# Tile 3's gram split by columns, and tile 2's layers moved ahead of its last rows, in a recommendation tower on one core

## The reference

```python
e = stack([tbl_f[ids[:, f]] for f in range(26)], axis=1)
T = concatenate([r_dense[:, None, :], e], axis=1)
Z = einsum('bnd,bmd->bnm', T, T)
z = Z[:, iu0, iu1]                       # upper triangle, 351 numbers
h = concatenate([z, r_dense], axis=1)    # 479
h = maximum(h @ W_top1 + b_top1, 0.0)    # 512
h = maximum(h @ W_top2 + b_top2, 0.0)    # 256
y = h @ W_top3                           # 1
```

## Time and profile before

| | us |
|---|---|
| median of 3 runs (lowest, highest) | 124.29 (123.7, 124.66) |
| the profiled execution's own time | 124.55 |
| its span in the trace | 122.6 |
| busy: PE, PE's weight load | 93.3, 76.8 |
| busy: DVE, ACT, POOL | 75.5, 73.7, 75.4 |
| mean granted clock of TensorE | 0.956 of full |

### The profile page before, as it was taken

How to read it: one execution, slowest core, us unless ns; L and a number is a source line. 1 busy time by engine, 2 the same in 40 slices (tenths; PEclk the granted TensorE clock), 3 DMA queues, 4 the chain that set the end, 5 groups by cost and what they waited for, 6 DMA issues and landing times. The chain is left out here.

```text
span 122.6 us, 3575 instructions
## 1 busy us (share of the span) xinstructions
PE 93.3 (76%) x1460; PEld 76.8 (63%) x1460; DVE 75.5 (62%) x164; ACT 73.7 (60%) x154; POOL 75.4 (62%) x82
## 2 busy tenths in 40 slices
PE   5659988979789879956519798787947666579791
PEld 5547755646557658756408697676937456569680
DVE  4979999999999995036350993119920104880422
ACT  4097799998799978378380997209942105860000
POOL 4888777887887887787878787777878600040000
PEclk9999999999999999998555999999999999999999
DMA  1896786969899831121222122121222100000000
GB/s 50 244 311 214 259 262 203 289 184 275 184 241 345 267 85 43 43 70 47 66 61 70 50 67 62 51 64 48 64 62 65 48 21 5 8 19 1 0 5 0
DMA packets 7452, 13.64 MB, mean 111 GB/s; under 512 B 2378, under 2 KB 4108, under 8 KB 7308
## 3 DMA queue, kind: packets, MB, share of 16 engines
q1 hardware_dynamic: 5068, 8.67, 22.6%
q0 software_dynamic: 2368, 4.74, 14.3%
HBM read 13.16 MB, written 0.00 MB: 107 GB/s over the span
## 5 line engine op out<-in xcount | busy, mean ns | idle before, releaser
L301 POOL DMA_INDIRECT rows<-tbl,idx x72 | 73.3, 1018 | 22.9 <-issue 21.6
L353 PE MATMUL l<-hot,t_hi 128*128 128x512 f32 x68 | 29.4, 433 | 6.2 <-DVE hot L537 3.8
L537 DVE TENSOR_TENSOR hot<-ids_bc,rownum 128x512 fp32r<-128x512 int32 x51 | 32.3, 693 | 0.4 <-PE l L355 0.4
L355 PE MATMUL l<-hot,t_lo 128*128 128x512 f32 x68 | 28.1, 414 | 0.0
L419 DVE COPY Zlow<-gr 14x224 f32<-14x224 f32 x16 | 8.6, 540 | 22.2 <-PE gr L370 22.0
L353 PEld LDWEIGHTS l<-hot,t_hi 128*128 128x128 f32 x68 | 13.7, 201 | 13.5 <-issue 7.9
L370 PE MATMUL gr<-XT 128*32 128x26 f32 x1024 | 14.8, 202 | 8.4 <-issue 4.9
L370 PEld LDWEIGHTS gr<-XT 128*32 128x32 f32 x1024 | 12.7, 117 | 11.2 <-issue 7.0
L502 ACT COPY XT<-tp 128x512 f32<-128x512 f32 (+1 forms) x20 | 12.2, 654 | 10.6 <-PE tp L341 10.5
L341 PE MATMUL tp<-ident,rows 128*128 128x128 f32 x72 | 11.4, 295 | 7.4 <-DMA rows<-tbl,idx 3.7
L419 ACT COPY Zlow<-gr 14x224 f32<-14x224 f32 x16 | 8.7, 545 | 13.1 <-PE gr L370 12.9
(11 more groups left out here) (32 smaller groups left out, 62.5 us busy)
## 6 DMA issues: line engine op xcount, KB each, us to landing
ids_bc<-ids_oh SPq DMA_DIRECT2D x8, 256.0 KB, 4.1
table<-small SPq DMA_DIRECT2D x4, 512.0 KB, 4.1
table<-small SPq DMA_DIRECT2D x2, 640.0 KB, 5.6
rows<-tbl,idx POOLq DMA_INDIRECT x72, 3.2
w_sb<-w SPq DMA_DIRECT2D x1, 1024.0 KB, 8.6
table<-small SPq DMA_DIRECT2D x2, 320.0 KB, 5.4
w_sb<-w SPq DMA_DIRECT2D x1, 512.0 KB, 8.2
table<-small SPq DMA_DIRECT2D x2, 192.0 KB, 4.9
```

The source lines that it names most:

```text
L301: nc.gpsimd.indirect_dma_start(rows[:, t, place - FIRST, :], None, tbls[f], bass.IndirectOffsetOnAxis(ap=idx[:, t, f:f + 1], axis=0)).then ...
L353: nc.tensor.matmul(lookup_bank(i), t_hi[:, i % PARTS, c * D:(c + 1) * D], hot[:, k % HOTS, :], start=c == 0, stop=False)
L355: last = nc.tensor.matmul(lookup_bank(i), t_lo[:, i % PARTS, c * D:(c + 1) * D], hot[:, k % HOTS, :], start=False, stop=c == n - 1)
L537: nc.vector.tensor_tensor(hot[:, k % HOTS, :], ids_bc[:, i % IDS, :], rownum[:, v, c:c + 1].broadcast_to((OH_ROWS, BATCH)), ALU.is_equal). ...
```

## The change

- The groups of every tile are now 4, 4, 4, 3 and 3 places.
- Tile 3's gram: `gram 3 h` takes places 0 to 20 alone and waits for the first three groups. Two new steps `late 3 h` follow when the last two groups are in: 64 matmuls each, weights of 27 places, six columns moving. Of the eight Zt copies of an engine for each half, four stay with the gram and four go to the late step. The five moves of Zlow wait for the first part alone.
- Tile 2's layers now stand ahead of tile 3's gram; tile 0's and 1's layers stand between grams and rows steps in a new order, each layer1 in two halves apart.
- Tile 3's dense part (`layer1 3 0`) follows the late matmuls and no longer has layer2 of tile 2 behind it. Blocks 0 and 1 go to the banks of `tp`.
- Tile 3's ReLUs are shared: DVE blocks 0 and 2, ACT 1 and 3; of the second layer's two one each.
- The weights of a gram are 27 (tile 3: 21) places, not 32.

```diff
-GROUPS = [(a, min(4, PLACES - a)) for a in range(FIRST, PLACES, 4)]
+LATE_QUADS = 2
+LATE = PLACES - LATE_QUADS * CHUNKS
+GROUPS = [(a, min(4, LATE - a)) for a in range(FIRST, LATE, 4)] + [(a, CHUNKS) for a in range(LATE, PLACES, CHUNKS)]
...
+    steps += [("rows", 1, 0), ("rows", 1, 1)]
+    steps += [("gram", 0, 0), ("rows", 1, 2), ("gram", 0, 1), ("rows", 1, 3), ("rows", 1, 4)]
+    steps += [("gram", 1, 0), ("rows", 2, 0), ("layer1", 0, 0), ("gram", 1, 1), ("layer1", 0, 1), ("rows", 2, 1),
+              ("layer2", 0, 0), ("rows", 2, 2), ("layer1", 1, 0), ("rows", 2, 3), ("layer1", 1, 1), ("rows", 2, 4)]
+    steps += [("gram", 2, 0), ("layer2", 1, 0), ("gram", 2, 1), ("rows", 3, 0), ("rows", 3, 1), ("layer1", 2, 0),
+              ("rows", 3, 2), ("layer1", 2, 1), ("layer2", 2, 0), ("gram", 3, 0), ("gram", 3, 1), ("rows", 3, 3), ("rows", 3, 4)]
+    steps += [("late", 3, 0), ("late", 3, 1), ("layer1", 3, 0), ("layer1", 3, 1), ("layer2", 3, 0)]
...
                 elif kind == "gram":
-                    pe.wait_ge(tp_empty, banks_filled(("rows", t, len(GROUPS) - 1)))
+                    pe.wait_ge(tp_empty, banks_filled(("rows", t, len(GROUPS) - 1 - (LATE_QUADS if t == TILES - 1 else 0))))
+                    n = LATE if t == TILES - 1 else PLACES
...
-                            last = nc.tensor.matmul(gr[PAD * s:PAD * (s + 1), halves % GRAM_BANKS, q, 0:FIELDS],
-                                                    XT[:, b, :], XT[:, b, 1:PLACES], start=True, stop=True)
+                            last = nc.tensor.matmul(gr[PAD * s:PAD * s + n, halves % GRAM_BANKS, q, 0:n - 1],
+                                                    XT[:, b, 0:n], XT[:, b, 1:n], start=True, stop=True)
...
+                elif kind == "late":
+                    pe.wait_ge(tp_empty, banks_filled(("rows", t, len(GROUPS) - 1)))
+                    pe.wait_ge(gram_dve, halves - GRAM_BANKS + 1)
+                    pe.wait_ge(gram_act, halves - GRAM_BANKS + 1)
+                    for q in range(QH):
+                        for s in range(SAMPLES):
+                            b = t * P + (i * SAMPLES + s) * QH + q
+                            last = nc.tensor.matmul(gr[PAD * s:PAD * s + PLACES, halves % GRAM_BANKS, q, 0:PLACES - LATE],
+                                                    XT[:, b, 0:PLACES], XT[:, b, LATE:PLACES], start=True, stop=True)
...
                 elif kind == "layer1" and t == TILES - 1 and i == 0:
                     pe.wait_ge(gram_dve, HALVES * TILES)
                     pe.wait_ge(gram_act, HALVES * TILES)
+                    pe.wait_ge(tp_empty, banks)
...
                 elif kind == "layer1" and t == TILES - 1:
+                    pe.wait_ge(gram_dve, HALVES * (TILES + 1))
+                    pe.wait_ge(gram_act, HALVES * (TILES + 1))
...
+                elif kind == "late":
+                    act.wait_ge(gram_full, halves + 1)
+                    copy_high(nc.scalar.copy, t, i, halves % GRAM_BANKS, range(SAMPLES - ACT_SAMPLES, SAMPLES),
+                              range(QUADS - LATE_QUADS, QUADS), LATE - 1).then_inc(gram_act, 1)
...
+                elif kind == "layer1" and t == TILES - 1 and i == 1:
+                    act.wait_ge(l2_full, t)
+                    for u in range(1, BLOCKS, 2):
+                        act.wait_ge(l1_full, t + 1 + u)
+                        nc.scalar.activation(h1[:, u, :], l1_block(t, u), ACT.Relu).then_inc(h1_act, 1)
```

More of the change, by code:

```diff
@@ L100, in timeline @@
         steps += [("rows", 0, g) for g in ROWS_AFTER.get(i, [])]
[L101 to L111, removed]
+    steps += [("rows", 1, 0), ("rows", 1, 1)]
[5 more added lines that the diff above has]
+    steps += [("late", 3, 0), ("late", 3, 1), ("layer1", 3, 0), ("layer1", 3, 1), ("layer2", 3, 0)]
+    return steps
 STEPS = timeline()
@@ L413, in _, with copy_low @@
                     last.then_inc(l3_full, 1)
-        def copy_gram(copy, t, h, half, samples, low_copied):
+        def copy_low(copy, t, h, bank, samples):
             for s in samples:
@@ L419, in copy_gram, with copy_high, early_quads @@
                 last = copy(Zlow[:, t % 2, :, first:first + QH].rearrange("n m q -> n q m"),
-                            gr[PAD * s:PAD * s + LOW, half, :, 0:LOW])
-            last.then_inc(low_copied, 1)
+                            gr[PAD * s:PAD * s + LOW, bank, :, 0:LOW])
+            return last
+        def copy_high(copy, t, h, bank, samples, quadrants, column):
             for s in samples:
                 first = t * P + (h * SAMPLES + s) * QH
-                for g, n in enumerate(HIGH_ROWS):
+                for g in quadrants:
+                    n = HIGH_ROWS[g]
                     last = copy(Zt[PAD * g:PAD * g + n, :, first:first + QH].rearrange("n c q -> n q c"),
-                                gr[PAD * s:PAD * s + n, half, :, n - CHUNKS:n])
+                                gr[PAD * s:PAD * s + n, bank, :, n - CHUNKS - column:n - column])
             return last
+        def early_quads(t):
+            return range(QUADS - (LATE_QUADS if t == TILES - 1 else 0))
         @block.scalar
@@ L505, in _ @@
                     banks += 1
+                elif kind == "layer1" and t == TILES - 1 and i == 1:
[3 more added lines that the diff above has]
+                        nc.scalar.activation(h1[:, u, :], l1_block(t, u), ACT.Relu).then_inc(h1_act, 1)
+                elif kind == "layer2" and t == TILES - 1:
+                    act.wait_ge(w2_in, 2 * 16)
+                    act.wait_ge(l3_full, t)
+                    act.wait_ge(l2_full, t + 1)
+                    nc.scalar.activation(h2[:, 1, :], l2_block(t, 1), ACT.Relu,
+                                         bias=tail_sb[:, 0, 1:2]).then_inc(h2_act, 1)
         @block.vector
@@ L545, in _ @@
                     dve.wait_ge(gram_full, halves + 1)
-                    copy_gram(nc.vector.tensor_copy, t, i, halves % GRAM_BANKS,
-                              range(SAMPLES - ACT_SAMPLES), low_dve).then_inc(gram_dve, 1)
+                    samples = range(SAMPLES - ACT_SAMPLES)
+                    copy_low(nc.vector.tensor_copy, t, i, halves % GRAM_BANKS, samples).then_inc(low_dve, 1)
+                    copy_high(nc.vector.tensor_copy, t, i, halves % GRAM_BANKS, samples, early_quads(t),
+                              0).then_inc(gram_dve, 1)
+                    halves += 1
+                elif kind == "late":
+                    dve.wait_ge(gram_full, halves + 1)
+                    copy_high(nc.vector.tensor_copy, t, i, halves % GRAM_BANKS, range(SAMPLES - ACT_SAMPLES),
+                              range(QUADS - LATE_QUADS, QUADS), LATE - 1).then_inc(gram_dve, 1)
                     halves += 1
@@ L555, in _ @@
                     else:
-                        for u in range(BLOCKS):
-                            dve.wait_ge(l1_full, units_ready(t, u))
+                        for u in range(0, BLOCKS, 2):
+                            dve.wait_ge(l1_full, t + 1 + u)
                             nc.vector.tensor_scalar(h1[:, u, :], l1_block(t, u), 0.0, None,
```

39 lines of the change are left out of this document (30 added, 9 removed).

## The result

| | median us | runs | lowest, highest |
|---|---|---|---|
| before | 124.47 | 4 | 123.70, 125.03 |
| changed | 139.16 | 4 | 137.14, 140.11 |

The ratio is 1.108 (95% interval 1.094 to 1.122): slower by 11%. I forecast 133.3, 7% slower, with a range to 138.0; the median lies 1.2 above it. Executions fall into a faster and a slower state, and the ratio is that of the faster runs (137.14 and 138.52 of the changed kernel, mean 137.8, just inside the range), while the profiled execution, 140.11, is the longest of the slower. In it y's last copy ends at 136.24 + 0.28 = 136.52.

What follows compares the result with a forecast made beforehand. Gathers were taken to set the first 100.5 us and a tail 20.6. The walk's 127.6, plus 2.2 for the low clock and 3.5 added to every end, gave 133.3 us, 7% slower; range 127.5 to 138.

Steps and rivals of the forecast that it cites:

- What bounds the kernel: Whole kernel: gathers set 100.5 us, a tail of 20.6 us follows; gathers end at the same 97.6 after the change.
- The code blocks: TensorE's code comes in blocks of some 126 pairs, each starting at least 3.4 to 3.7 us after the one before.
- Rival 2: Tile 3's second gram and second late part: code arrives in time, no holes; 126.8 us, 129.0 with low clock; 12%.
- The walk: TensorE's list followed step by step in the new order, from gram (1,0) to y's end at 127.6 us.
- Grams at 1.35 us: Each gram of 128 pairs in tiles 2 and 3 was counted at about 1.35 us.
- I take no hole here: Gram (2,1): no wait for code, ending at 91.8; block before began at about 88.3, + 3.4 = 91.7.
- rival 3: Third hole in gram (2,1), + 2.0, and longer idle with low clock into layer2, + 2: 135.5 to 137.5 us; 22%.
- if the fetch is later, as it can be after waits: Gram (2,1): a later code fetch would cost up to 2 us; none was counted.
- The low clock, 2.2 us: Layers behind the new 5.2 us idle stretch (93 to 98.2) run at 1.2 GHz; price 0 to 4.4, middle 2.2.
- h2's shared ReLU: From tile 3's pairs to y's end: sharing saves 0.3 us, making 6.1 instead of 6.4.
- the cost of the late parts: Behind tile 3's gram: part one 1.3 us, part two ends at 119.9 with its hole; holes cost full 2.1 each.
- Rival 1: Tail gets short, tile 2's layers and tile 3's gram done by 100.6: y at 114.1, 117.6 us; 7% faster.

Runs made afterwards that it cites:

- the held pair: Kernel before and changed kernel, each with POOL waiting for the last one-hot lookup before gathering for tiles 2 and 3: 124.20 and 138.27 us.
- shift_blocks: Changed kernel with 2 warm-up transposes instead of 16; ratio 1.070 to the kernel before, on a slow chip.
- held_changed: Changed kernel with POOL waiting for the last one-hot lookup before gathering for tiles 2 and 3: 138.27 us, ratio 1.111 to the kernel before.
- order_only: Kernel before with the new order of steps, no split: 203.9 against 187.5 us on a slow chip, ratio 1.092; repeated, 1.099.
- keep_busy: Changed kernel with five filler matmuls in the idle stretch ahead of layer1 (2,0): ratio 1.099 to the kernel before, on a slow chip.
- held_interleaved: interleaved with POOL waiting for the last one-hot lookup before gathering for tiles 2 and 3: 122.38 us, ratio 0.983 to the kernel before.
- held_split_old_order: Changed kernel with the old list apart from tile 3's gram and late parts, plus POOL's wait for the last lookup: 128.52 us, ratio 1.029 to before.
- interleaved: Changed kernel reordered so no two grams stand together, layer2 (2) between the late parts: 187.5 against 189.1 us before, slow chip, ratio 0.997.
- Held_order_only: Kernel before with the new order, no split, and POOL's wait for the last lookup: 198.7 against 183.0 us on a slow chip.

## Why the prediction was right, and where it was short

*What bounds the kernel.* Right. The gathers started their last at 96.57, as before; the tail grew by 15.6 us (84.4 against 68.8) in these two profiles, by 14.1 in the held pair.

*The code blocks.* Right in the places: all three holes in grams lie where the count put them (177 pairs into tile 3's two grams, forecast 128 + 48; 169 into the late parts, forecast 128 + 38), 1.67 to 2.23 us long, and shift_blocks moved them by the 14 pairs that it took away. Rival 2, the Trainium skill's "mostly hidden" (Runtime: NRT & Kernel Launch, Instruction fetch mechanics), falls. The rate was less right. The 3.4 to 3.7 us from one block's start to the next fit the holes of tile 3 (about 3.4), but the hole at 83.88 before comes only some 3.0 us after its block began (44 pairs into gram (2,0), by the pace of its rows about 80.9), and that of gram (2,1) 6.2 us after (89.99 to 96.17).

*The walk.* In the profiled execution each mark came, late by a growing amount: gram (2,0) 86.3 against 84.7, end of gram (2,1) 96.5 against 91.8, layer1 (2,0) 103.0 against 98.2, gram (3,0) 113.8 against 107.2, end of the second late part 127.0 against 119.9, y 136.5 against 127.6 (129.8 with the clock's 2.2). That is 6.7 us more than the sum; the two quicker runs of the result were 4.5 above it and have no profile. Held_changed's profile (138.92) has the same three holes at 1.33, 2.22 and 1.15 us, so their lengths vary between executions. The terms mis-sized:

- Grams at 1.35 us. That was the pace of the gram behind the last gather; beside gathers 128 pairs took 1.6 to 1.8 (the rows at 70.86 and 86.33). I had 14 ns a pair as the upper bound and took none of it. The low clock also ran longer, over layer1 (0,0), which took 3.2 us (67.62 to 70.86) instead of 2.2. That is 1.0 of the 1.6 us by gram (2,0).
- "I take no hole here" in gram (2,1): the step that failed most. The hole came, 1.67 us, 11 pairs before the end, as in rival 3; with the gram's own pace this step was 2.3 us longer. Layer2 (1) ahead of it was 0.8 longer (the copies that its ReLU waits behind began 2.3 us after gram (2,0) did, not 1.4). With the 1.6 carried that makes 4.7 us at the end of gram (2,1).

  What was wrong is the moment of the fetch, which I put at the start of the block before ("at about 88.3, + 3.4"). That block began at 89.99, and PE then waited for h2 until 92.39. The queue of kind "instruction" moved nothing from 89.5 to 93.3, and one packet between 93.3 and 93.6 (`q8 instruction: 1, 0.02, 27.3%`). So the next block was fetched only once PE was past the wait, and could be used 3.8 us after it (92.39 to 96.17). The same wait and the same hole give 4.1 in order_only (158.07 to 162.13), 3.8 in keep_busy (156.48 to 160.26) and 3.5 in held_changed (91.92 to 95.43). The prediction had this as "if the fetch is later, as it can be after waits", and gave it no time.
- The low clock, 2.2 us. Layer1 (2) with rows (3,2) took 102.99 to 109.85, 6.9 us, 2.0 more than the 4.9 at full clock, near the value taken. The reason given, the new idle stretch, isn't shown: the clock fell at its very start, and in held_changed at 93.3, inside gram (2,1) (PEclk 1.00 from 92.00 to 93.20, 0.50 from 93.40 to 95.40). And a second low stretch came at 118.2 and lasted until 131.9 (PEclk 1.00 from 108.10 to 118.20, 0.50 from 118.30 to 131.80). Tile 3's pairs took 128.94 to 133.02, 4.1 us, against 2.7 in held_interleaved (113.93 to 116.62): 1.4 more. One low stretch was priced, and there were two. The second began behind the hole at 117.94; held_split_old_order has one from inside the hole of its late parts on (PEclk 0.50 from 111.20 to 113.90), and held_interleaved, without that hole, has none there. That the holes bring it is an inference.
- h2's shared ReLU and the cost of the late parts (both holes near full length) were as forecast: from gram (3,0) to their end 13.3 us against 12.7.

Of the rivals, 3 (135.5 to 137.5) came nearest, and it is what happened: the third hole and a longer low clock, to which I gave 22% against the 55% of the forecast itself. So the direction and the way of the loss were foreseen; that the time still lay in the range, and narrowly, is partly luck: the sum was 4.5 us short, and only the range reached to this rival. The range's lower end, 127.5, should have been rival 2's 126.8. Rival 1, a short tail, is what interleaved reaches in part: not with the changed kernel's list.

## What to carry to other kernels

Work moved "ahead" in one in-order list moves all else back: ask which step starts the longest chain outside the engine (here gram (2,1), with 6.5 us of copies, DMAs and landing behind it, 96.46 to 102.99) and put nothing ahead of that. Splitting a step of many tiny matmuls to shorten the last part doubles its instructions, and where code arrives in blocks this is paid in holes, unless other work with few instructions stands between. Count instructions as well as microseconds.

## What the runs showed of the hardware

A block of some 126 pairs of TensorE's code came about 3.0 to 3.7 us after the block before it began where a hole shows it (3.0 at 83.88 before, 3.7 at 59.71), and 14 instruction pairs taken away far ahead moved the place of every later hole. Where TensorE waited for another engine seven pairs behind a block's start, the next block came 5.5 to 6.2 us after that start, 3.5 to 4.1 after the wait. A wait ten pairs behind the start (the block of 59.31 in the changed kernel, waiting until 63.62) did not hold the fetch back: its packet came between 60.5 and 60.8. At full clock, grams of 128 pairs took 1.87 us beside gathers and 1.25 behind them (held_interleaved, 84.39 and 101.77, the latter with 20 columns instead of 26), and 1.29 in order_only at 152.65, with 26 columns and also behind them. That the gathers slow the issue is an inference from these times. On a slow chip the grams all but stop beside gathers. Held_order_only starts its gathers for tiles 2 and 3 at 71.5 us, and from there PE's grams crawl, for stretches one pair every 2.8 us, until the gathers are over (last start 115.3):

```profile
113.72 0.20 PE L369 MATMUL gr<-XT 128*32 128x26 f32 x1 [2.60 <-issue]
116.52 0.20 PE L369 MATMUL gr<-XT 128*32 128x26 f32 x1 [2.60 <-issue]
...
122.12 1.73 PE L369 MATMUL gr<-XT 128*32 128x26 f32 x110 [0.45 <-issue]
```

In the kernels without POOL's wait the one-hot part ended only after the gathers there. Why work beside gathers nearly stands still on some chips and not on others wasn't tried and stays open.
